# Transformer block on one core: four projections as single f32 products of unsplit operands

## The chip, the cores and the metric

The kernel runs on one core of a Trainium2 chip. The metric is the device time of one execution in microseconds (us). The core has five engines that run side by side and wait for each other through semaphores: TensorE (PE, matrix products; its weight loads are shown as PEld), VectorE (DVE), ScalarE (ACT), GpSimd (POOL) and SyncE (SP, which issues transfers).

## The reference

`x` is 16 x 112 rows of 256 numbers, `ctx` 16 x 375 rows of 192. The block is a cross attention with 16 heads of 16 numbers, followed by a mixture of 8 experts of which each row takes two; both are added to `x` behind a gate.

```python
q = (layernorm(x) @ Wq)            # 16 batches, 112 x 256
k = ctx @ Wk                       # 16 batches, 375 x 256
v = ctx @ Wv
attn = softmax(q @ k.T / 4)        # for each batch and head
x = x + tanh(g_xattn) * ((attn @ v) @ Wo)
# then, for each row of layernorm(x): router, top 2 of 8 experts
y = sum_e probs[e] * ((silu(x @ gate_w[e] + gate_b[e]) * (x @ up_w[e] + up_b[e])) @ down_w[e] + down_b[e])
x = x + tanh(g_ffn) * y
```

The change touches the four products with Wq, Wk, Wv and Wo.

## The kernel before, in words

`build` runs two parts in turn, `attention` and `experts`. Each engine has a program of its own, written out in order; between engines there are only semaphores.

**Two number formats.** TensorE takes 4-byte operands in two ways. As `F32R` (fp32r) a product is one matmul instruction of reduced precision. As `F32` the builder issues two weight loads and two matmul instructions for one `pe.matmul`. The kernel before gets its precision out of fp32r by splitting: an operand is written as a high part (the fp32r copy) and a low part (the operand less its high part), and a product is three: high x high, low x high, high x low. The weights are split once (`w_high` on ACT, `w_low` on DVE, tiles `wk_h`, `wk_l` and so on); the transposed context is split for each batch (`cTH` on ACT, `cTL` on DVE, `transposed`), so are the transposed attention outputs (`oTH`, `oTL`), and the normalised `x` for each group of four batches (`xTH`, `xTL`).

**The start.** SP loads the weights, the first contexts and X. PE projects K and V of batch 0; DVE takes the statistics of X. Then, for four groups of four batches, PE transposes normalised rows into `psO` (`turn`, L687) and multiplies them by Wq (L707: `wq_h` and `wq_l` with `xTH` and `xTL`, 448 columns), ACT copies the results to `qH`, DVE makes `qL`, and SP writes both to `q_scr` in memory. `turn(g + 1)` may write `psO` when `s_xl` says that DVE has read it for `xTL`.

**The steps.** After that come 19 steps, one for each batch and three to drain. Step n projects K and V of batch n (`project_k` L542, `project_v` L552), takes the scores of batch n-1 and their row maxima (`scores` L566 on PE, `maximum` L732 on DVE), takes the transposed scores of batch n-2 again with the maximum subtracted (`scores_T` L581), their exponentials (ACT L468), the low parts of these (`low`: DVE L722 or POOL L346) and their products with V (`sums` L600), multiplies batch n-3 by Wo (`project_o` L637) and routes batch n-4 (L621, L628). A step has 15 slots, and each engine walks through them in this written order: on PE, K stands in slots 1 and 2 (`KP`), V in slots 4 to 6 (`VP`), the transpose of the maxima (`max_T`, L572) in slot 8, the transpose of the next context (`ctx_T` L532) in slot 10, Wo in slot 12.

**The loops between engines.** Scores use two banks in turn, so that `scores` of head h waits for the maximum of head h-2. V shares the tile `misc` with K: `project_v` waits for `v_K`, the end of DVE's `kL` (L786), which follows ACT's `kH` (L481), which follows the second half of K. SP writes `kH` and `kL` to `k_scr` (L271), waits until they have landed and loads them back, arranged by head, as `KS` (L275, 3 transfers of 376 KB). Behind these it issues the row of negative maxima, `nm` (DVE L796 after `max_T`), into `QS` (L304); the first `scores_T` of the next step waits for it:

```python
                    if k == 0:
                        pe.wait_ge(d_m[u], 16 * (h + 1))
```

So one step runs from `max_T` over the slots 9 to 14 (the tail) to the first `scores_T` of the next step, and over its slots 0 to 8 (the head) to the next `max_T`.

## Time and profile before

| | us |
|---|---|
| median of 3 runs | 670.81 |
| lowest and highest of them | 664.48, 671.11 |
| the profiled execution | 665.95 |
| its span, first to last instruction | 664.2 |

The span is one execution as the hardware profiler saw it; 1.75 us of the profiled execution lie outside it. Its stages: the start up to 57 us, the attention steps from 57 to about 366 us, the routing up to 456 us, the tiles of the experts up to the end. The lowest and the highest of the three runs lie 1% apart, and the profiled execution is near the lowest, so a time that is worked out from the profiled execution has to be moved by 4.9 us to stand beside the median.

### The profile page before, as it was taken

The page shows a single profiled execution, that of the slowest core. Times are in us where ns is not written, and L with a number is a line of the kernel's source. Part 1 is how long each engine was busy: PE and PEld are TensorE (multiplying, and loading weights), DVE is VectorE, ACT ScalarE, POOL GpSimd, SP SyncE. Part 2 cuts the span into 40 slices and gives each one's busy share as a digit, 9 for nine tenths or more (in the row PEclk, how much of TensorE's full clock was granted, in tenths as well). Part 3 has the DMA queues.
Part 4 walks back from the last instruction along what each step waited for, and adds up shares of the span by engine and source line. Part 5 has one row for each costly group of instructions (what it writes and reads, how often), then busy time and mean ns, then how long its engine had stood idle before and what let it go on. Part 6 is the DMA issues. An engine that isn't in the chain of part 4 may idle for free. (4 is left out here: it accounts for less than half of the span.)

```text
span 664.2 us, 15005 instructions
## 1 busy us (share of the span) xinstructions
PE 489.1 (74%) x4678; PEld 441.6 (66%) x4679; DVE 428.0 (64%) x896; ACT 329.3 (50%) x600; POOL 290.5 (44%) x238
## 2 busy tenths in 40 slices
PE   3368579898899999899988400004999999999950
PEld 2366478788788888788877300003899999999940
DVE  1755388887789998799888589710555555555520
ACT  1332255666557766657656552501555555555520
POOL 9301255553355555454547037871133333333340
PEclk9998599998899999899989755556999999999995
DMA  8448665688687877767530394934143334333224
GB/s 181 128 101 211 153 146 136 193 236 232 152 228 213 229 175 224 230 175 200 127 84 2 112 349 153 353 100 156 41 65 60 61 62 63 57 58 59 34 33 126
DMA packets 84360, 94.64 MB, mean 143 GB/s; under 512 B 27128, under 2 KB 72912, under 8 KB 84128
## 3 DMA queue, kind: packets, MB, share of 16 engines
q1 hardware_dynamic: 76736, 84.92, 46.5%
q0 software_dynamic: 7584, 9.21, 9.1%
q8 instruction: 23, 0.38, 0.3%
q14 instruction: 17, 0.14, 0.1%
HBM read 60.99 MB, written 34.83 MB: 144 GB/s over the span
## 5 line engine op out<-in xcount | busy, mean ns | idle before, releaser
L346 POOL TENSOR_TENSOR PL<-PT 125x448 f16<-125x448 f32 x96 | 100.3, 1048 | 146.5 <-ACT PT L468 146.4
L732 DVE TENSOR_REDUCE mx<-bank 112x1 f32<-112x375 f32 x256 | 130.6, 542 | 43.5 <-PE bank L566 41.3
L468 ACT ACTIVATE PT<-bank 125x448 f32<-125x448 f32 x192 | 103.8, 544 | 91.3 <-PE bank L581 90.6
L1286 POOL DMA_INDIRECT acc_scr<-ys,where x42 | 65.2, 1552 | 131.9 <-ACT ys L1318 122.9
L566 PE MATMUL bank<-KS,QS 97*112 97x376 f32 x256 | 90.6, 378 | 13.5 <-DVE mx L732 11.0
L581 PE MATMUL bank<-QS,KS 98*125 98x256 f32 x384 | 83.9, 303 | 15.1 <-DMA QS<-nm 14.3
L581 PEld LDWEIGHTS bank<-QS,KS 98*125 98x125 f32 x384 | 66.7, 193 | 17.4 <-DMA QS<-nm 10.2
L1335 PE MATMUL bank<-ident,xt 128*128 128x128 f32 x84 | 13.5, 289 | 71.7 <-PEq L954 71.7
L1349 PE MATMUL bank<-xH,GH 128*128 128x256 f16 x336 | 64.7, 274 | 0.9 <-DVE xL L1381 0.6
L1349 PE MATMUL bank<-xL,GH 128*128 128x256 f16 x336 | 64.6, 274 | 0.0
L1349 PE MATMUL bank<-xH,GL 128*128 128x256 f16 x336 | 64.4, 273 | 0.0
L566 PEld LDWEIGHTS bank<-KS,QS 97*112 97x112 f32 x256 | 46.5, 185 | 25.0 <-DVE mx L732 20.8
L1389 DVE SCALAR_TENSOR_TENSOR hf<-bank,ub,sg 128x256 f32<-128x256 f32 x84 | 38.6, 481 | 38.0 <-ACT sg L1308 38.0
L722 DVE TENSOR_TENSOR PL<-PT 125x448 f16<-125x448 f32 x96 | 57.7, 618 | 3.0 <-ACT PT L468 2.6
L1335 PEld LDWEIGHTS bank<-ident,xt 128*128 128x128 f32 x84 | 10.1, 148 | 72.4 <-DMA xt<-xs_scr 72.0
L1308 ACT ACTIVATE sg<-bank,gb,inv 128x256 f32<-128x256 f32 x84 | 42.7, 559 | 30.2 <-PE bank L1349 30.1
L600 PE MATMUL bank<-VS,PT 125*128 125x49 bf16 x768 | 51.2, 186 | 2.8 <-DVE PL L722 2.1
L600 PE MATMUL bank<-VS,PL 125*128 125x49 bf16 x768 | 49.7, 184 | 0.0
L600 PEld LDWEIGHTS bank<-VS,PT 125*128 125x128 bf16 x768 | 38.7, 99 | 12.7 <-DVE PL L722 2.4
L1037 POOL DMA_INDIRECT xs_scr<-xn,pos x32 | 41.1, 1285 | 10.6 <-issue 7.6
L1393 DVE TENSOR_TENSOR hL<-hf,hH 128x1024 fp32r<-128x1024 f32 x21 | 25.7, 1225 | 23.7 <-ACT hH L1313 23.7
L1318 ACT ACTIVATE ys<-ys,where 128x256 f32<-128x256 f32 x42 | 19.0, 500 | 41.7 <-DVE ys L1401 41.7
(202 smaller groups left out, 1123.7 us busy)
## 6 DMA issues: line engine op xcount, KB each, us to landing
KS<-k_scr SPq DMA_DIRECT2D x48, 376.0 KB
k_scr<-kH SPq DMA_DIRECT2D x16, 376.0 KB, 2.5
k_scr<-kL SPq DMA_DIRECT2D x16, 376.0 KB, 3.7
xs_scr<-empty SPq DMA_DIRECT2D x9, 645.0 KB, 9.0
xt<-xs_scr SPq DMA_DIRECT2D x21, 258.0 KB, 2.8
QS<-q_scr SPq DMA_DIRECT2D x96, 56.0 KB, 5.0
ctx_sb<-in_ctx SPq DMA_DIRECT2D x16, 281.2 KB
wsq<-in_L_ffn_gate_w SPq DMA_DIRECT2D x8, 512.0 KB, 4.6
```

The costliest lines, as they stand in the source:

```text
L346: pool.tensor_tensor(PL[:, 2 * k:2 * k + 2, :, 0:N], PT[:, 2 * k:2 * k + 2, :, 0:N], PH[:, 2 * k:2 * k + 2, :, 0:N], ALU.subtract).then_in ...
L468: act.activation(PT[:, 2 * k:2 * k + 2, :, 0:N].rearrange("p a e i -> p (a e) i"), psST[k % 2][0:JP].rearrange("p (a i) -> p a i", i=NI)[: ...
L566: pe.matmul(psS[hd % 2][0:N, 0:MP], QS[u][0:RM, hd // 2, hd % 2, 0:N], KS[u][0:RM, hd // 2, :], start=True, stop=True).then_inc(p_S, 1)
L581: mm = pe.matmul(psST[k % 2][0:JP, 2 * NI * a:2 * NI * (a + 1)], KS[u][0:RM + 1, p, JP * t:JP * (t + 1)], QS[u][0:RM + 1, p, :, :].rearran ...
L600: mm = pe.matmul(psO[hd // 8][:, VW * (hd % 8):VW * (hd % 8 + 1)], P[:, JT * p + t, e, :], VS[:, u, t, hd, :], start=(part == 0 and t == 0 ...
L722: dve.tensor_tensor(PL[:, 2 * k:2 * k + 2, :, 0:N].rearrange("p a e i -> p (a e) i"), PT[:, 2 * k:2 * k + 2, :, 0:N].rearrange("p a e i -> ...
L732: dve.tensor_reduce(mx[:, hd:hd + 1], psS[hd % 2][0:N, 0:M], AX.X, ALU.max).then_inc(v_max, 1)
L1037: pool.indirect_dma_start(xs_scr, bass.IndirectOffsetOnAxis(ap=pos[k][:, b:b + 1].bitcast(mybir.dt.uint32), axis=0), xn[:, b, :], None).th ...
L1286: pool.indirect_dma_start(acc_scr, bass.IndirectOffsetOnAxis(ap=where[:, t % UN, k, 0:1].bitcast(mybir.dt.uint32), axis=0), ys[:, u, k, :] ...
L1308: act.activation(sg[:, f, :], bG[f // FB][:, TS * (f % FB):TS * (f % FB + 1)], ACT.Silu, bias=gb[:, bass.ds(e * FC + f, 1)], scale=inv[:, ...
L1349: mm = pe.matmul(bank[:, TS * (f % FB):TS * (f % FB + 1)], w.rearrange("p o f -> p (o f)"), x[:, u, k, :], start=(n == 0 and k == 0), stop ...
L1389: dve.scalar_tensor_tensor(out=hf[:, f, :], in0=bU[f // FB][:, TS * (f % FB):TS * (f % FB + 1)], scalar=ub[:, bass.ds(e1 * FC + f, 1)], in ...
```

## The change

The weights stay as loaded, in `Wf`, now kept for the whole of the attention part, and the products take them and the unsplit `cT`, `xT` and `oT` as `F32`. Every product of three pairs of fp32r instructions becomes one of two `pe.matmul` calls (one for each half of the contraction), each of which is issued as two matmul instructions with a weight load each. The splitting steps of ACT and DVE are gone: `w_high`, `w_low`, DVE's `transposed`, `oTL` and `xTL`. PE waits for ACT's copy in their place (`a_T`, `a_O`, `s_xc`), and for the transfers of the weights. The scale 1/4 of the queries moves from the weights to `q_high` and `q_low`, where DVE's subtraction becomes a `scalar_tensor_tensor` of the same size. The split of q and k for the scores stays.

```diff
-        WH = {k: sb(f"w{k}_h", [p, 2, DIM], F32R) for k, (_, p) in shapes.items()}
-        WL = {k: sb(f"w{k}_l", [p, 2, DIM], F32R) for k, (_, p) in shapes.items()}
+        Wf = {k: sb(f"w{k}_f", [p, 2, DIM], F32) for k, (_, p) in shapes.items()}
...
-        cTH = sb("cTH", [CK, 2, MP], F32R)
-        cTL = sb("cTL", [CK, 2, MP], F32R)
+        cT = sb("cT", [CK, 2, MP], F32)
...
-        xTH = first("xTH", [128, 2, 2, GB * N], F32R)
-        xTL = first("xTL", [128, 2, 2, GB * N], F32R)
+        xT = first("xT", [128, 2, 2, GB * N], F32)
...
-        oTH = sb("oTH", [128, 2, N], F32R)
-        oTL = sb("oTL", [128, 2, N], F32R)
+        oT = sb("oT", [128, 2, N], F32)
...
-                def w_high(k):
-                    act.wait_ge(s_w[k], 16)
-                    act.activation(WH[k][:], Wf[k][:], ACT.Copy, scale=SCALE if k == "q" else 1.0).then_inc(s_wh, 1)
...
-                w_high("k")
-                w_high("v")
                 transposed(0, 0)
                 act.wait_ge(s_g, 32)
                 act.activation(tg[:], gates[:], ACT.Tanh).then_inc(s_tg, 1)
-                w_high("q")
-                w_high("o")
...
-                        act.activation(qH[:, g, c, :], (psS, psST)[g % 2][c][:, 0:GB * N], ACT.Copy
-                                       ).then_inc(s_qh, 1)
+                        act.activation(qH[:, g, c, :], (psS, psST)[g % 2][c][:, 0:GB * N], ACT.Copy,
+                                       scale=SCALE).then_inc(s_qh, 1)
...
-                        act.activation(xTH[:, g % 2, c, :], psO[c][:, 0:GB * N], ACT.Copy).then_inc(s_xh, 1)
+                        act.activation(xT[:, g % 2, c, :], psO[c][:, 0:GB * N], ACT.Copy).then_inc(s_xc, 1)
...
-                        pe.wait_ge(v_T, b + 1)
-                    for n, (w, r) in enumerate(((WH, cTH), (WL, cTH), (WH, cTL))):
-                        for k in range(2):
-                            mm = pe.matmul(misc[:, 512 * m:512 * m + MP], w["k"][:, k, m * 128:(m + 1) * 128],
-                                           r[:, k, :], start=(n == 0 and k == 0), stop=(n == 2 and k == 1))
+                        pe.wait_ge(a_T, b + 1)
+                    for k in range(2):
+                        mm = pe.matmul(misc[:, 512 * m:512 * m + MP], Wf["k"][:, k, m * 128:(m + 1) * 128],
+                                       cT[:, k, :], start=(k == 0), stop=(k == 1))
...
-                    for n, (w, r) in enumerate(((WH, cTH), (WL, cTH), (WH, cTL))):
-                        for k in range(2):
-                            mm = pe.matmul(misc[0:JP, DIM * t:DIM * (t + 1)], r[:, k, JP * t:JP * (t + 1)],
-                                           w["v"][:, k, :], start=(n == 0 and k == 0), stop=(n == 2 and k == 1))
+                    for k in range(2):
+                        mm = pe.matmul(misc[0:JP, DIM * t:DIM * (t + 1)], cT[:, k, JP * t:JP * (t + 1)],
+                                       Wf["v"][:, k, :], start=(k == 0), stop=(k == 1))
...
-                    pe.wait_ge(v_O, b + 1)
-                    for n, (w, r) in enumerate(((WH, oTH), (WL, oTH), (WH, oTL))):
-                        for k in range(2):
-                            mm = pe.matmul(psS[0][0:N, 0:DIM], r[:, k, :], w["o"][:, k, :],
-                                           start=(n == 0 and k == 0), stop=(n == 2 and k == 1))
+                    pe.wait_ge(a_O, b + 1)
+                    for k in range(2):
+                        mm = pe.matmul(psS[0][0:N, 0:DIM], oT[:, k, :], Wf["o"][:, k, :], start=(k == 0), stop=(k == 1))
...
-                pe.wait_ge(s_wl, 2)
+                pe.wait_ge(s_w["k"], 16)
+                pe.wait_ge(s_w["v"], 16)
...
-                        pe.wait_ge(s_xl, g)
+                        pe.wait_ge(s_xc, 2 * g)
...
-                pe.wait_ge(s_wl, 3)
+                pe.wait_ge(s_w["q"], 16)
...
-                    pe.wait_ge(s_xl, g + 1)
+                    pe.wait_ge(s_xc, 2 * g + 2)
...
-                        for n, (w, r) in enumerate(((WH, xTH), (WL, xTH), (WH, xTL))):
-                            for c in range(2):
-                                mm = pe.matmul((psS, psST)[g % 2][m][:, 0:GB * N],
-                                               w["q"][:, c, m * 128:(m + 1) * 128], r[:, g % 2, c, :],
-                                               start=(n == 0 and c == 0), stop=(n == 2 and c == 1))
+                        for c in range(2):
+                            mm = pe.matmul((psS, psST)[g % 2][m][:, 0:GB * N], Wf["q"][:, c, m * 128:(m + 1) * 128],
+                                           xT[:, g % 2, c, :], start=(c == 0), stop=(c == 1))
...
-                pe.wait_ge(s_wl, 4)
+                pe.wait_ge(s_w["o"], 16)
...
-                def transposed(i, c):
-                    b, h, u = at(i, c)
-                    dve.wait_ge(a_T, b + 1)
-                    dve.tensor_tensor(cTL[:, :, 0:M], misc[0:CK].rearrange("p (c n) -> p c n", c=2)[:, :, 0:M],
-                                      f32(cTH[:, :, 0:M]), ALU.subtract).then_inc(v_T, 1)
...
-                        if s == OT + 1 and live(i, c, 3):
-                            b, h, u = at(i, c - 3)
-                            dve.wait_ge(a_O, b + 1)
-                            dve.tensor_tensor(oTL[:], psS[0][:, 0:2 * N].rearrange("p (c i) -> p c i", c=2),
-                                              f32(oTH[:]), ALU.subtract).then_inc(v_O, 1)
...
-                        if s == CT + 1 and live(i, c, -1) and not starts(i, c):
-                            transposed(i, c + 1)
...
-                def w_low(k, n):
-                    dve.wait_ge(s_wh, n)
-                    dve.scalar_tensor_tensor(out=WL[k][:], in0=Wf[k][:], scalar=SCALE if k == "q" else 1.0,
-                                             in1=f32(WH[k][:]), op0=ALU.mult, op1=ALU.subtract).then_inc(s_wl, 1)
-
-                w_low("k", 1)
-                w_low("v", 2)
-                transposed(0, 0)
...
-                w_low("q", 3)
-                w_low("o", 4)
...
-                        ins = dve.tensor_tensor(qL[:, g, c, :], (psS, psST)[g % 2][c][:, 0:GB * N],
-                                                f32(qH[:, g, c, :]), ALU.subtract)
+                        ins = dve.scalar_tensor_tensor(out=qL[:, g, c, :], in0=(psS, psST)[g % 2][c][:, 0:GB * N],
+                                                       scalar=SCALE, in1=f32(qH[:, g, c, :]), op0=ALU.mult,
+                                                       op1=ALU.subtract)
...
-                    dve.wait_ge(s_xh, 2 * g + 2)
-                    if g >= 2:
-                        dve.wait_ge(s_qp, g - 1)
-                    for c in range(2):
-                        ins = dve.tensor_tensor(xTL[:, g % 2, c, :], psO[c][:, 0:GB * N], f32(xTH[:, g % 2, c, :]),
-                                                ALU.subtract)
-                    ins.then_inc(s_xl, 1)
...
-                    if g == 1:
-                        transposed(0, 1)
```

On TensorE, in slots 1 and 2 of a step inside the loop: scores and transposed scores between the two halves of K. Before:

```order
L581 MATMUL bank<-QS,KS 125x256 x2
L542 MATMUL misc<-cTH,wk_h 128x376 x2
L542 MATMUL misc<-cTH,wk_l 128x376 x2
L542 MATMUL misc<-cTL,wk_h 128x376 x2
L566 MATMUL bank<-KS,QS 112x376 x2
```

With the change:

```order
L566 MATMUL bank<-QS,KS 125x256 x2
L526 REGISTER_ALU
L528 MATMUL misc<-cT,wk_f 128x376 x2
L232 REGISTER_ALU
L551 MATMUL bank<-KS,QS 112x376
```

Nothing has moved: the three pairs of fp32r products of a half of K are one pair of f32 products at the same place, in front of the same scores.

On VectorE, in the tail of a step inside the loop, from the negative maxima to the update of X. Before:

```order
L796 TENSOR_SCALAR nm<-bank 16x112
...
L746 TENSOR_TENSOR on<-osum,rden 112x128
L776 TENSOR_TENSOR oTL<-bank,oTH 128x224
...
L722 TENSOR_TENSOR PL<-PT 125x4x112
L752 REGISTER_ALU
L753 TENSOR_TENSOR cTL<-misc,cTH 96x2x375
L721 REGISTER_ALU
L722 TENSOR_TENSOR PL<-PT 125x4x112
L801 ISA
```

With the change:

```order
L767 TENSOR_SCALAR nm<-bank 16x112
...
L728 TENSOR_TENSOR on<-osum,rden 112x128
...
L704 TENSOR_TENSOR PL<-PT 125x4x112
L703 REGISTER_ALU
L704 TENSOR_TENSOR PL<-PT 125x4x112
L772 ISA
```

The two subtractions are gone from between the low parts of the exponentials; the rest keeps its order.

## Rows read from the trace of the kernel before

**Rows 1.** The page: busy time of the engines; TensorE's clock in 40 slices.

```profile
PE 489.1 (74%) x4678; PEld 441.6 (66%) x4679; DVE 428.0 (64%) x896; ACT 329.3 (50%) x600; POOL 290.5 (44%) x238
...
PEclk9998599998899999899989755556999999999995
```

**Rows 2.** The instructions of L572, one a step: duration, first and last start.

```profile
L572 PE MATMUL bank<-ident,mx x16: 262/263/354, 70.5 to 353.8; 112*16 112x112 f32 x16
```

**Rows 3.** Busy time by stretches: length, engines, clock, DMA share, GB/s; a tail, a head.

```profile
209.20:214.20 5.00, 4.81 (x75) 4.33 (x75) 4.81 (x12) 3.09 (x8) 1.28 (x1) 1.00 1.08 227
214.20:227.10 12.90, 11.74 (x112) 10.62 (x112) 11.48 (x24) 9.65 (x17) 7.99 (x8) 1.00 0.79 244
```

**Rows 4.** Waits of PE from 137.5 to 299 us: total, times, longest.

```profile
PE bank L566 <- DVE mx L732: 5.0, 15, 0.6
PE bank L581 <- DMA QS<-nm: 4.7, 4, 1.4
```

**Rows 5.** Timeline of PE, half of K and the scores behind it.

```profile
215.14 0.51 PE L542 MATMUL misc<-cTH,wk_h 96*128 96x376 f32 x2
...
215.84 0.50 PE L542 MATMUL misc<-cTL,wk_h 96*128 96x376 f32 x2
216.17 0.50 PE L566 MATMUL bank<-KS,QS 97*112 97x376 f32 x2
```

**Rows 6.** Timeline of PE, third of V and the scores behind it.

```profile
220.06 0.50 PE L552 MATMUL misc<-wv_h,cTH 96*125 96x256 f32 x2
...
220.64 0.40 PE L552 MATMUL misc<-wv_h,cTL 96*125 96x256 f32 x2
220.88 0.34 PE L566 MATMUL bank<-KS,QS 97*112 97x376 f32 x1
```

**Rows 7.** Timeline of DVE, tail and head of one step.

```profile
210.74 0.39 DVE L776 TENSOR_TENSOR oTL<-bank,oTH 128x224 fp32r<-128x224 f32 x1
...
212.17 0.94 DVE L753 TENSOR_TENSOR cTL<-misc,cTH 96x750 fp32r<-96x750 f32 x1
213.02 0.61 DVE L722 TENSOR_TENSOR PL<-PT 125x448 f16<-125x448 f32 x1
...
219.07 0.93 DVE L786 TENSOR_TENSOR kL<-misc,kH 128x752 fp32r<-128x752 f32 x1
...
221.26 1.00 DVE L732 TENSOR_REDUCE mx<-bank 112x1 f32<-112x375 f32 x2 [0.34 <-PE bank L566]
```

**Rows 8.** Timeline: f32 products of the routing; fp32r products at the start.

```profile
13.45 0.83 PE L542 MATMUL misc<-cTH,wk_l 96*128 96x376 f32 x2
...
14.08 0.83 PE L542 MATMUL misc<-cTL,wk_h 96*128 96x376 f32 x2
...
384.29 0.63 PE L1080 MATMUL bank<-r_exp,ones 112*112 112x128 f32 x2
```

**Rows 9.** Groups of PE's instructions by shape: busy time, mean ns of one.

```profile
L1080 PE MATMUL bank<-r_exp,ones 112*112 112x128 f32 x2 | 0.6, 421 | 0.0
```

**Rows 10.** Busy time and clock of the stretch that holds L1080.

```profile
380.00:390.00 10.00, 1.61 (x6) 1.16 (x6) 8.27 (x15) 7.31 (x5) 5.56 (x2) 0.50 1.07 372
```

**Rows 11.** Tile nm: who waited for it (us, times), its transfers from issue to landing.

```profile
  PE bank L581: 14.3, 9
...
DMA to landing us min/median/max: 1.7/4.4/6.6
```

**Rows 12.** Timeline of SP's issues: the loads of KS and nm behind them.

```profile
206.30 1.31 SPq L275 DMA_DIRECT2D KS<-k_scr  x3
209.90 0.56 SPq L304 DMA_DIRECT2D QS<-nm  x1
```

**Rows 13.** Timeline of the start: query products and the wait for xTL.

```profile
40.26 0.56 PE L707 MATMUL bank<-xTH,wq_l 128*128 128x448 f32 x2
...
40.66 0.57 PE L707 MATMUL bank<-xTL,wq_h 128*128 128x448 f32 x2
...
47.39 1.04 PE L687 MATMUL bank<-ident,xn 112*128 112x112 f32 x8 [4.30 <-DVE xTL L864]
```

More of the change, by code:

```diff
@@ L120, in attention @@
         first = lambda name, shape, dt: early.enter_context(nc.sbuf_tensor(name, shape, dt))
-        Wf = {k: first(f"w{k}_f", [p, 2, DIM], F32) for k, (_, p) in shapes.items()}
         mask_sb = first("mask_sb", [B, M], U8)
@@ L148, in attention @@
         s_id0, s_id = sem("ident_zero"), sem("ident_ready")
-        s_clear, s_wh, s_wl, s_bias = sem("cleared"), sem("w_high"), sem("w_low"), sem("bias_ready")
+        s_clear, s_bias = sem("cleared"), sem("bias_ready")
         s_st, s_mv, s_ve, s_sq, s_rs = (sem(n) for n in ("ln_stats", "ln_mv", "ln_veps", "ln_sqrt", "ln_rstd"))
-        s_xn, s_xt, s_xh, s_xl = sem("xn_ready"), sem("xT_ready"), sem("xT_high"), sem("xT_low")
+        s_xn, s_xt, s_xc = sem("xn_ready"), sem("xT_ready"), sem("xT_copied")
         s_qp, s_qh, s_ql = sem("q_psum"), sem("q_high"), sem("q_low")
@@ L176, in attention @@
         a_T, a_K, a_V, a_V1, a_V2, a_E, a_O = (sem(n) for n in ("act_ctxT", "act_k", "act_v", "act_v1", "act_v2", "act_exp", "act_oT"))
-        v_T, v_K, v_L, v_max, v_nm = (sem(n) for n in ("dve_ctxT", "dve_k", "dve_plow", "dve_max", "dve_negmax"))
-        v_os, v_rd, v_on, v_O, v_x1 = (sem(n) for n in ("dve_osum", "dve_rden", "dve_on", "dve_oT", "dve_x1"))
+        v_K, v_L, v_max, v_nm = (sem(n) for n in ("dve_k", "dve_plow", "dve_max", "dve_negmax"))
+        v_os, v_rd, v_on, v_x1 = (sem(n) for n in ("dve_osum", "dve_rden", "dve_on", "dve_x1"))
         g_r, g_V, g_L = (sem(n) for n in ("pool_rest", "pool_v", "pool_plow"))
@@ L237, in wait @@
                 eng.wait_ge(s, value)
-        constants = [(f32(cTH[:, :, M:MP]), 0.0), (f32(cTL[:, :, M:MP]), 0.0), (bias_sb[:, M:MP], 0.0),
+        constants = [(cT[:, :, M:MP], 0.0), (bias_sb[:, M:MP], 0.0),
                      (VS[:, :, :, :, VW - 1:VW].rearrange("p u t h o -> p (u t) h o"), 1.0)]
@@ L405, in transposed @@
                         wait(act, p_V, JT * b)
-                        act.activation(cTH[:, :, 0:M], misc[0:CK].rearrange("p (c n) -> p c n", c=2)[:, :, 0:M],
+                        act.activation(cT[:, :, 0:M], misc[0:CK].rearrange("p (c n) -> p c n", c=2)[:, :, 0:M],
                                        ACT.Copy).then_inc(a_T, 1)
@@ L457, in slots @@
                             wait(act, p_Wo, b)
-                            act.activation(oTH[:], psS[0][:, 0:2 * N].rearrange("p (c i) -> p c i", c=2),
+                            act.activation(oT[:], psS[0][:, 0:2 * N].rearrange("p (c i) -> p c i", c=2),
                                            ACT.Copy).then_inc(a_O, 1)
```

## The prediction

> **What bounds the kernel now.** I read the page first. TensorE is the busiest engine, VectorE stands not far behind, and neither is full [rows 1]. The change touches the start and the attention steps alone; routing and experts run the same code. Then the steps: L572 stands in each once, 16 times from 70.5 to 353.8 us, so a step lasts 283.3 / 15 = 18.9 us [rows 2]. The two stretches of one such step show in its head of 12.9 us 11.74 us of PE and 11.48 us of DVE, in its tail of 5.0 us 4.81 us of each, with the transfer engines full all through the tail (share 1.08) [rows 3]. No single engine bounds it; the question is which hand-over comes last, slot by slot. The waits answer it in part: in 161 us PE waits 15 times for a maximum, 5.0 us in total, and 4 times for the transfer of `nm`, up to 1.4 us [rows 4].
>
> In the tail the transfers decide. The loads of KS are issued at 206.3 us, `nm` behind them at 209.9 us [rows 12]. `nm` is 7 KB and needs a median of 4.4 us to land, up to 6.6; PE waits for it in 9 of 16 steps, 14.3 us in total [rows 11]. In the step of the rows it lands at about 214.1 us, 0.1 us before the first `scores_T`. So in 9 steps the chain kL, k_scr, KS, nm sets when the next head begins, and in the other steps the tail's own work ends at nearly the same time.
>
> In the head PE sets the pace in slots 1, 2 and 4 to 6, where K and V stand in front of the scores. DVE is idle there for 0.34 us until PE has passed a third of V and the score behind it [rows 6, 7].
>
> **The price of an f32 product.** In the routing the second of two f32 products of 128 columns shows 0.63 us for two matmul instructions of 0.421 us each [rows 8, 9], so they follow each other by 0.63 - 0.42 = 0.21 us, at a granted clock of 0.50, 1.2 GHz [rows 10]: 1.64 ns a column. The fp32r products at 13.45 us follow each other by (14.08 - 13.45) / 2 = 0.315 us for 376 columns, 0.84 ns a column [rows 8]; that is 1.8 times what the same product takes at 215 us, so I take PE's clock for halved there too, though the page's row shows no drop. An f32 instruction thus costs two fp32r instructions of the same width, and there are two of it for each `pe.matmul`. Three fp32r products become one that costs four. At full clock:
>
> - K: a pair takes 0.35 us [rows 5], one 0.175. Half of K: 6 x 0.175 = 1.05 us before, 4 x 0.33 to 0.35 = 1.32 to 1.40 with the change. I take +0.30 us for each half, +0.60 for both.
> - V: a pair takes 0.24 us (220.64 to 220.88) [rows 6], one 0.12. A third of V: 0.72 before, 4 x 0.23 = 0.92 with the change: +0.20, three thirds +0.60.
> - Wo: the same width and count as a third of V, +0.20.
> - Wq: a pair takes 0.40 us [rows 13], one 0.20 for 448 columns. A group: 12 x 0.20 = 2.4 before, 8 x 0.39 = 3.1 with the change, +0.7, four groups +2.8.
>
> The Trainium skill says the same by another way, "FP8 and Floating Point Precision", TensorE Precision Notes: a true FP32 product is four passes through the array. By it the four replace three passes, and K's 1.05 us would be an estimated 1.40; the rows above give 1.32 to 1.40.
>
> **What goes.** On DVE, for each step, `oTL` 0.39 us and `cTL` 0.94 us [rows 7], with its successors overlapping by 0.1 each: 1.15 us. At the start, four weight splits, 8 `xTL` and two `cTL`. On ACT four weight copies, which stood beside loads. `oTL` and `cTL` both lie in the tail, not in the head where PE is paced.
>
> **The head of a step.** K's second half ends 0.6 us later, so `kH`, `kL` and V begin 0.6 us later; `kL` starts 219.07 in the step of the rows, behind the maximum of head 5, which itself waits for PE then. V adds 0.2 in each of three slots; DVE, which waited 0.34 us at 221.26 [rows 7], waits longer and has no work to bring forward, since the scores are in PE's order behind V. So the head grows by 1.2 us. Cover for it would be PE's waits for maxima, 5.0 us in 9 steps [rows 4], 0.55 a step; they lie in slots 3, 7 and 8, after the added work, where DVE is the late one. Where DVE was late it now gets its scores 1.2 us later too, so little of this cover counts; I take 0.1 of it: +1.1 us.
>
> **The tail.** DVE's last low part there starts at 213.02, right after `cTL` [rows 7], and the last `sums` wait for it. Without `cTL` they could start 0.4 us earlier. Wo's +0.2 falls before the router, whose input comes from ACT; between 0 and 0.2 of it counts, and I take 0.1. So the tail's own work shrinks by 0.2 to 0.3 us. Where `nm` decides, nothing of this counts, but the chain gives something else: it starts with kL, before V, so V's 0.6 us pass while the transfers run. Such a step grows by K's 0.6 us alone. That gives 9 steps x 0.6 = 5.4 us and 6 steps x (1.1 - 0.25) = 5.1 us: +10.5 us for the 15 steps with K and V.
>
> **The start.** Wq's +2.8 us stands on PE's path to the first scores, V of batch 0 with 18 fp32r instructions at half clock adds 3 x 0.4 = 1.2 us before `turn`. Against it: DVE's splits of wq and wo in front of the first `normal`, by the width of `cTL` (750 columns in 0.94 us [rows 7]) 0.64 us each for 512; `turn(1)` and `turn(3)` wait for ACT's copy and not for `xTL` behind it. PE waits 4.30 us for `xTL` at 47.39 us [rows 13], and that chain (cTL, normal, xTL) loses two of its three DVE steps, some 1 to 2 us. Sum: between -1.5 and +1.5 us, I take 0. In the first steps, up to 93 us, the clock is low (the fifth of the page's 40 slices, 66 to 83 us, stands at 5 tenths, the fourth at 8 [rows 1]), and K and V cost up to double the extra: +1 us, mostly under the first long wait for `nm`.
>
> **Sum.** 665.95 + 10.5 + 0 + 1 = 677.5 us on the profiled execution's own time. That execution lies 4.9 us below the median of the runs shown. Moved by these, the median of the changed kernel should be 682 us, +1.7%.
>
> **The rivals.**
>
> *Hidden in the transfer chain: 674 us (chance 0.24).* All steps are bound by kL, KS and nm, and V is free in all; PE's waits for `nm` are halved in length, so the clock drops after them go as well. Between 83 and 350 us four of the page's slices of 16.6 us stand at 8 tenths where the others have 9 [rows 1]; a tenth of such a slice is 1.7 us. 15 x 0.6 = 9, +1 at the start, less 4 x 1.7 = 6.8: +3 us. For it: transfers are full in the tail, `nm` takes a median of 4.4 us. Against: in 6 of the steps PE had no wait for it.
>
> *DVE's relief decides: 657 us (0.06).* If DVE is the engine that is late in most slots, the 1.15 us that it loses shorten the step: 15 x 1.15 = 17 less, +1 to 4 given back by Wq. For it: 16.3 us of DVE in a step of 17.9 [rows 3]. Against: the 1.15 us lie in the tail, and `nm` would have to land 1 us earlier. It decides if `nm`'s landing after its issue falls under 3.5 us everywhere.
>
> *An f32 instruction is no dearer than an fp32r one: 643 us (0.05).* Then K costs 4 x 0.175 a half and the head loses 2 x 0.35 + 3 x 0.24 = 1.4 us a step, DVE's part comes on top in part: 15 x 1.6 = 24 us, and 4 us of Wq. The rows at half clock speak against it: 0.21 us for 128 columns would have to be 0.11. They are of 112 weights and 128 columns, so a weight load that takes as long could hide a cheaper stream; that is all there is for it. The Trainium skill, "Perfetto Trace Analysis", Engine Utilization, gives FP32_LOW_HIGH half the output rate of the array; read as the rate of the whole product, this is that rival, read as that of each of the two instructions it is my price.
>
> *PE becomes the bound everywhere: 693 us (0.10).* The whole 1.2 us of the head and 0.2 of Wo count in 15 to 18 steps, 22 us, with no relief in the tail, since kL and with it `nm` come later in step: this is the slow side of my own case.
>
> **How the numbers follow.** My case, 682 us, has 0.55: on its own it reaches from 676 to 689. 1% (6.7 us) is about what a measurement of this kernel can tell from no change. Slower by over 1% are my case but for its lowest tenth and the last rival: 0.49 + 0.10, and a fifth of the first rival, 0.05: 0.64. Within 1%: the rest of those two, 0.25. Faster: 0.11. The range 668 to 692 leaves out the two fast rivals and the upper half of the last one.
>
> **What would show it.** Right: K's instructions at L528 follow each other by 0.33 to 0.35 us at full clock, V's by 0.22 to 0.24; DVE's wait for PE in slots 2 and 5 grows by 0.2 to 0.3 each; a step (L572's successor) lasts 0.7 us more on the mean; PE's waits for `nm` shrink. Wrong: a spacing near 0.17 us; steps that grow by more than 1.2 us (then kL has pushed KS into the next step); or a start that ends more than 2 us from 57 us. The clock is the weakest point: PE is busier, so dips may vanish, and each is worth 1 to 2 us.

## The result, and the profile after

| | before | after |
|---|---|---|
| median, us | 668.72 (4 runs, 664.48 to 671.11) | 680.16 (4 runs, 674.51 to 685.33) |
| ratio, 95% interval | | 1.0172 [1.0103, 1.0242] |
| the profiled execution, us | 665.95 | 685.33 |
| its span, us | 664.2 | 683.5 |

The change costs 1.7%, 11.4 us between the medians. A second measurement of the same kernel, beside 17 runs of the kernel before, gave 1.0127 [1.0055, 1.0200], with a median of 677.84 us (6 runs). The profiled execution of the first measurement is the longest of its four and was left out of the ratio, so sums of the whole are made with the profile of the second one, 674.29 us with a span of 672.5.

The page of the kernel after, to be held against [rows 1]:

```profile
PE 517.5 (76%) x4470; PEld 431.7 (63%) x4471; DVE 405.5 (59%) x852; ACT 327.8 (48%) x596; POOL 288.4 (42%) x237
...
PEclk9997599999989999999996855555899999999995
```

PE has 28 us more to do in fewer instructions (21 us in the second measurement), DVE 22.5 us less. The product rows of the attention steps, PE's timeline of after, half of K and a third of V, each with the scores behind it (before: [rows 5, 6]):

```profile
223.04 1.43 PE L528 MATMUL misc<-cT,wk_f 96*128 96x376 f32 x4
224.02 0.79 PE L551 MATMUL bank<-KS,QS 97*112 97x376 f32 x2
...
231.83 1.03 PE L537 MATMUL misc<-wv_f,cT 96*125 96x256 f32 x4
232.51 0.52 PE L551 MATMUL bank<-KS,QS 97*112 97x376 f32 x1
```

A matmul begins before the one ahead of it has ended. One instruction of 376 columns in fp32 lasts 0.48 us by itself, so four of them spaced by s last 0.48 + 3s = 1.43: s = 0.317 us, where an fp32r one took 0.175. For 256 columns (1.03 - 0.38) / 3 = 0.217, where fp32r took 0.12. So half of K costs 1.27 us instead of 1.05 (+0.22), and a third of V 0.87 instead of 0.72 (+0.15).

The same two stretches of a step as in [rows 3], tail and head, with the same columns:

```profile
217.50:222.14 4.64, 4.64 (x74) 4.06 (x74) 3.67 (x10) 3.09 (x8) 1.23 (x1) 1.00 1.01 247
222.14:235.50 13.36, 12.62 (x108) 10.06 (x104) 11.12 (x24) 9.65 (x17) 8.00 (x8) 1.00 0.73 208
```

The tail has lost 0.36 us and DVE's work in it 1.14; the head is 0.46 us longer and PE's work in it 0.88. This step takes 18.00 us where the one of before took 17.90. DVE's timeline shows what stands where the relief was (before: [rows 7]):

```profile
218.96 1.15 DVE L704 TENSOR_TENSOR PL<-PT 125x448 f16<-125x448 f32 x2
220.85 0.62 DVE L704 TENSOR_TENSOR PL<-PT 125x448 f16<-125x448 f32 x1 [0.73 <-ACT PT L463]
...
229.78 1.00 DVE L714 TENSOR_REDUCE mx<-bank 112x1 f32<-112x375 f32 x2 [0.49 <-PE bank L551]
```

Where `cTL` stood DVE now waits 0.73 us for ACT's exponentials. In the head its wait for a third of V has grown from 0.34 to 0.49 us, by what that third costs.

That the head grew by 0.46 us and not by 0.88 has another reason, on DVE in slot 7: `xc`, the centring of a routed batch, beside POOL's low part, before and then after.

```profile
224.47 0.94 POOL L346 TENSOR_TENSOR PL<-PT 125x448 f16<-125x448 f32 x1 [0.26 <-ACT PT L468]
...
224.71 0.84 DVE L765 TENSOR_SCALAR xc<-X,mv 112x256 f32 x1
```

```profile
232.85 0.93 POOL L341 TENSOR_TENSOR PL<-PT 125x448 f16<-125x448 f32 x1 [0.25 <-ACT PT L463]
...
233.54 0.39 DVE L741 TENSOR_SCALAR xc<-X,mv 112x256 f32 x1
```

From the start of the head to `xc` it was 10.51 us and is 11.40: PE's added work counts in full. Then `xc`, which began 0.24 us behind POOL's instruction and took 0.84 us, begins 0.69 behind it and takes 0.39, and gives 0.45 us back. (The 0.34 us that `xc` takes in some other steps is its shortest.)

But the steps together grew by more than this one. The maxima's transposes, one a step, of after and then of its second measurement (before: [rows 2]):

```profile
L557 PE MATMUL bank<-ident,mx x16: 263/264/356, 71.9 to 370.8; 112*16 112x112 f32 x16
```

```profile
L557 PE MATMUL bank<-ident,mx x16: 263/263/356, 70.4 to 364.7; 112*16 112x112 f32 x16
```

15 steps take 298.9 and 294.3 us where they took 283.3: +1.0 and +0.7 a step. The tile `nm` of after (before: [rows 11]) shows PE's waits for it as they were:

```profile
  PE bank L566: 15.7, 9
...
DMA to landing us min/median/max: 1.8/4.2/7.0
```

And the start, from PE's timeline of after (before: [rows 13]): the wait for `xTL`, 4.30 us, has become one of 1.84 for ACT's copy, and the steps' first scores stand at 55.51 us, 1.6 before those of the kernel before (57.07).

```profile
46.26 0.96 PE L671 MATMUL bank<-ident,xn 112*128 112x112 f32 x8 [1.84 <-ACT xT L503]
...
55.51 0.96 PE L551 MATMUL bank<-KS,QS 97*112 97x376 f32 x2 [2.26 <-DVE qL L809]
```

### The profile page after: what moved, and what is told of

It is laid out like the page before. It is cut to its first block and busy times, and to the rows that moved or that the text cites. A ratio compares the mean times of both kernels' runs of the same rounds, so it can differ in the third digit from the quotient of the medians.

```text
span 683.5 us, 14536 instructions
## 1 busy us (share of the span) xinstructions
PE 517.5 (76%) x4470; PEld 431.7 (63%) x4471; DVE 405.5 (59%) x852; ACT 327.8 (48%) x596; POOL 288.4 (42%) x237
## 5 line engine op out<-in xcount | busy, mean ns | idle before, releaser
L551 PE MATMUL bank<-KS,QS 97*112 97x376 f32 x256 | 109.5, 451 | 13.7 <-DVE mx L714 10.5
L566 PE MATMUL bank<-QS,KS 98*125 98x256 f32 x384 | 86.9, 312 | 16.3 <-DMA QS<-nm 15.7
L566 PEld LDWEIGHTS bank<-QS,KS 98*125 98x125 f32 x384 | 69.1, 201 | 22.0 <-DMA QS<-nm 11.7
L537 PE MATMUL misc<-wv_f,cT 96*125 96x256 f32 x192 | 55.8, 418 | 10.4 <-DVE kL L757 9.1
L528 PE MATMUL misc<-cT,wk_f 96*128 96x376 f32 x128 | 55.0, 561 | 1.0 <-ACT cT L401 1.0
L585 PEld LDWEIGHTS bank<-VS,PT 125*128 125x128 bf16 x768 | 40.2, 102 | 11.8 <-issue 2.1
L537 PEld LDWEIGHTS misc<-wv_f,cT 96*125 96x125 f32 x192 | 35.8, 200 | 17.1 <-DVE kL L757 13.3
```

Of the source, the lines that this page charges most:

```text
L528: mm = pe.matmul(misc[:, 512 * m:512 * m + MP], Wf["k"][:, k, m * 128:(m + 1) * 128], cT[:, k, :], start=(k == 0), stop=(k == 1))
L537: mm = pe.matmul(misc[0:JP, DIM * t:DIM * (t + 1)], cT[:, k, JP * t:JP * (t + 1)], Wf["v"][:, k, :], start=(k == 0), stop=(k == 1))
L551: pe.matmul(psS[hd % 2][0:N, 0:MP], QS[u][0:RM, hd // 2, hd % 2, 0:N], KS[u][0:RM, hd // 2, :], start=True, stop=True).then_inc(p_S, 1)
L566: mm = pe.matmul(psST[k % 2][0:JP, 2 * NI * a:2 * NI * (a + 1)], KS[u][0:RM + 1, p, JP * t:JP * (t + 1)], QS[u][0:RM + 1, p, :, :].rearran ...
L585: mm = pe.matmul(psO[hd // 8][:, VW * (hd % 8):VW * (hd % 8 + 1)], P[:, JT * p + t, e, :], VS[:, u, t, hd, :], start=(part == 0 and t == 0 ...
```

## The experiments

For each profiled run the table has the start up to the first transpose of the maxima, the 15 steps up to the last one, the rest of the span, and the ratio of the timed runs to the kernel before. "Before" and "after" stand for the kernel that was edited. A single profile stands behind each row: where nothing differs, the rest still lies between 307.8 and 313.6, and the 15 steps of after and after_again, the same kernel, differ by 4.6 us. A difference of a few us between two rows of steps shows nothing by itself.

| run | start | 15 steps | rest | ratio, 95% interval |
|---|---|---|---|---|
| before | 70.5 | 283.3 | 310.4 | |
| after | 71.9 | 298.9 | 312.7 | 1.0172 [1.0103, 1.0242] |
| after_again | 70.4 | 294.3 | 307.8 | 1.0127 [1.0055, 1.0200] |
| dve_relief (before) | 66.9 | 280.8 | 311.6 | 0.9906 [0.9862, 0.9950] |
| pe_price (after) | 69.2 | 292.1 | 310.8 | 1.0121 [1.0049, 1.0192] |
| one_product (before) | 56.4 | 289.6 | 311.6 | 0.9892 [0.9822, 0.9962] |
| ks_cut_before | 71.1 | 266.9 | 310.9 | 0.9756 [0.9692, 0.9819] |
| ks_cut_after | 71.9 | 276.9 | 308.6 | 0.9803 [0.9725, 0.9881] |
| f32_k (before) | 69.1 | 284.5 | 310.6 | 1.0060 [1.0018, 1.0103] |
| kv_split (before) | 71.1 | 284.4 | 312.1 | 0.9967 [0.9928, 1.0006] |
| f32_v (before) | 73.0 | 291.3 | 310.2 | 1.0209 [1.0107, 1.0312] |
| nm_act_before | 70.1 | 330.2 | 313.6 | 1.0698 [1.0587, 1.0810] |
| nm_act_after | 71.3 | 329.4 | 310.6 | 1.0548 [1.0381, 1.0715] |
| after_xc9 | 70.8 | 288.0 | 311.3 | 1.0046 [1.0004, 1.0089] |

**after_again**: the changed kernel, measured a second time beside the next three.

> The changed kernel once more, for a ratio with a narrower interval and a second trace of it. Theory (K and V pace the heads, the transfer of nm ends the tails): 1.012 to 1.022 times the kernel before, steps 0.7 us longer on the mean, and the steps without a wait for nm longer by less than 0.7 us, since in the first trace one of them grew by 0.1 us only. Rival (the change is worth nothing, the 1.7% were scatter): under 1.007.

**dve_relief**: the change's relief of DVE without its cost on PE. `cTL`, `oTL` and `xTL` are not made, PE waits for ACT's copies (`v_O` and `s_xl` are replaced in the same way), and the weights' low parts stay.

```diff
-                    pe.wait_ge(v_T, b + 1)
-                    for n, (w, r) in enumerate(((WH, cTH), (WL, cTH), (WH, cTL))):
+                    pe.wait_ge(a_T, b + 1)
+                    for n, (w, r) in enumerate(((WH, cTH), (WL, cTH), (WH, cTH))):
```

> The kernel before, with VectorE's subtractions cTL, oTL and xTL left out; the third product of each projection takes the high part in place of the low one, so TensorE's work is that of before (the low parts are missing from the result). This is the relief of VectorE alone. Theory: nothing in the tails where nm ends them, 0.25 us in the others, and 2 to 3 us at the start, where turn waits for xTL: 3 to 5 us less than before, ratio 0.993 to 0.996. Rival (VectorE decides the steps): 15 x 1.15 = 17 us less, ratio 0.975.

**pe_price**: the change's cost on PE, with two of DVE's subtractions kept and PE waiting for them as before (`oTL` with `v_O` in the same way as `cTL`).

```diff
-                        pe.wait_ge(a_T, b + 1)
+                        pe.wait_ge(v_T, b + 1)
...
+                    dve.tensor_tensor(cTL[:, :, 0:M], misc[0:CK].rearrange("p (c n) -> p c n", c=2)[:, :, 0:M],
+                                      cT[:, :, 0:M], ALU.subtract).then_inc(v_T, 1)
```

> The changed kernel with VectorE's subtractions of the context and of the attention outputs put back (into tiles that nobody multiplies), and TensorE waiting for them as before; the f32 products stay. This is TensorE's price with the steps' relief of VectorE taken away. Theory: the relief in the steps was worth 1 to 3 us, so it is 1.018 to 1.025 times the kernel before. Rival (VectorE decides the steps): 17 us on top of the changed kernel, 1.042.

The transposes of the maxima, of dve_relief and of pe_price:

```profile
L572 PE MATMUL bank<-ident,mx x16: 263/264/354, 66.9 to 347.7; 112*16 112x112 f32 x16
```

```profile
L560 PE MATMUL bank<-ident,mx x16: 263/264/356, 69.2 to 361.3; 112*16 112x112 f32 x16
```

By the timed runs dve_relief is 0.9% faster, 6.3 us (3.4 to 9.3), somewhat more than the 3 to 5 us expected. In its profile 3.6 us of it lie in the start; the steps are shorter by 0.17 us each (280.8 against 283.3), which is within what two profiles of one kernel differ by. Giving 1.3 us of work in each step back to DVE in the changed kernel costs nothing: pe_price is 1.012 where the changed kernel beside it is 1.013, and the 1 to 3 us that I had expected the relief of the steps to be worth did not show. What the change costs in the steps comes from PE's side.

**one_product**: PE's products of all four projections cut to a third; no low parts are made for them.

```diff
-                    for n, (w, r) in enumerate(((WH, cTH), (WL, cTH), (WH, cTL))):
+                    for n, (w, r) in enumerate(((WH, cTH),)):
```

> The kernel before with one fp32r product of the high parts in place of three (the low parts are left out of the result), and no low parts made. TensorE loses 2.7 us of K and V in each head and 0.5 us of Wo in the tail, VectorE 1.15 us. Theory: the heads fall to what VectorE's 11.5 us allow, 1.0 to 1.4 us less a step, the tails stay with the transfer of nm, and the start loses 4 us: 19 to 25 us less than before, ratio 0.963 to 0.972. Rival (TensorE alone is the bound): 15 x 3.3 = 50 us less, 0.925. Rival (the transfers are the bound of every step, from kL to nm): K alone counts, 15 x 1.37 = 20 us, which does not tell from the theory by the time; the trace tells, by the waits for nm.

The page's clock of one_product, and its busy time in the first step and in the 14 behind it (columns as in [rows 3]):

```profile
PEclk9985577858959777969966655556999999999985
```

```profile
56.40:84.90 28.50, 15.92 (x99) 13.84 (x99) 10.54 (x21) 11.39 (x17) 15.20 (x14) 0.52 0.63 157
84.90:346.00 261.10, 234.13 (x2250) 198.83 (x2250) 212.05 (x458) 165.76 (x326) 136.24 (x113) 0.79 0.69 184
```

and the same 14 steps of the kernel before:

```profile
92.40:353.80 261.40, 233.75 (x2564) 209.62 (x2564) 224.41 (x484) 164.81 (x326) 132.62 (x113) 0.97 0.70 185
```

The start gains 14.1 us, of which the first step gives 6.6 back in a wait of PE for ACT's copy of V. The other 14 steps take 261.1 us instead of 261.4, with 314 matmul instructions less: PE is busy just as long, since its granted clock has fallen from 0.97 to 0.79. So PE's work is no simple price either: with a part of it taken out, the clock was lower. I had expected 19 to 25 us less than before, and it was 7 (0.9892).

**ks_cut_before, ks_cut_after**: two of the three transfers that load KS are left out in both kernels.

```diff
-                    for s, part in enumerate((0, 0, 1)):
+                    for s, part in enumerate((0,)):
...
-                        pe.wait_ge(d_ks[u], 64 * (h + 1))
+                        pe.wait_ge(d_ks[u], 32 * (h + 1))
```

> The kernel before with two of the three loads of KS from k_scr left out in each step (752 of 1128 KB; their rows keep the ones of the start, so the scores are others). The transfers between kL and nm get shorter. Theory (the loads of KS hold nm back, and nm ends the tail in half of the steps): no waits for nm after the first, steps of 17.5 to 18 us throughout, 12 to 18 us less than before, ratio 0.973 to 0.982. Rival (the transfers are beside the point, the long steps come from TensorE's clock): the long steps stay, within 4 us of before.

> The changed kernel with the same two loads of KS left out. With the transfers out of the way only what the engines do can differ between the kernels. Theory: the steps differ by what the undisturbed steps of the traces show, 0.1 to 0.7 us each, and the start by 1.5 us less, so the time is 0 to 9 us over that of ks_cut_before. Rival (TensorE's 1.1 us counts in full in every head): 15 us over it.

The tile `nm` of ks_cut_before, and then its transposes of the maxima and those of ks_cut_after:

```profile
  PE bank L581: 2.4, 1
...
DMA to landing us min/median/max: 1.7/1.8/3.1
```

```profile
L572 PE MATMUL bank<-ident,mx x16: 262/263/264, 71.1 to 338.0; 112*16 112x112 f32 x16
```

```profile
L557 PE MATMUL bank<-ident,mx x16: 262/263/280, 71.9 to 348.8; 112*16 112x112 f32 x16
```

Two things follow. The chain behind KS is real: without two thirds of it `nm` lands in 1.8 us instead of 4.4, PE waits for it once, and the kernel before gains 2.4%. And the change does not hide behind it: with the chain out of the way the 15 steps of the profiles still grow by 10.0 us, as they do with it (11.0 in after_again). The timed runs, four of each, agree in the sign only: 657.51 against 652.11 us, with ratios whose intervals meet. The cause had to be elsewhere, and these two profiles, where almost no wait for `nm` blurs the steps, show where. Three of the 15 steps, each third one inside the loop, grow from 17.38 to 19.35 us, together 5.9 of the 10.0. Of the other twelve ten change by -0.95 to +0.5, and two grow by 1.6 and 1.5. One of the three, busy time by stretches, in ks_cut_before and then in ks_cut_after:

```profile
158.80:176.20 17.40, 16.54 (x188) 14.84 (x188) 15.82 (x36) 11.09 (x23) 9.90 (x9) 1.00 0.54 158
```

```profile
160.80:180.10 19.30, 17.26 (x175) 14.12 (x175) 15.99 (x34) 11.07 (x23) 10.57 (x9) 1.00 0.49 134
```

DVE has two instructions less, yet it is busy for 0.17 us longer. One of its instructions has grown.

**f32_k, f32_v**: the kernel before with K alone, or V alone, as one f32 product of the high parts; every splitting step stays.

```diff
-                    for n, (w, r) in enumerate(((WH, cTH), (WL, cTH), (WH, cTL))):
-                        for k in range(2):
...
+                    for k in range(2):
+                        mm = pe.matmul(misc[:, 512 * m:512 * m + MP], f32(WH["k"][:, k, m * 128:(m + 1) * 128]),
+                                       f32(cTH[:, k, :]), start=(k == 0), stop=(k == 1))
```

> The kernel before with K alone as one f32 product, of the high parts (the low parts of K are left out of the result); all of VectorE's work stays, V, Wo and Wq stay split. TensorE spends 2 x 0.23 us more in each head, before kL. Theory: K stands in front of the chain kL, KS, nm and so counts in every step: 15 x 0.46 = 7 us, ratio 1.007 to 1.012, that is the larger half of the change. Rival (any work of TensorE counts alike, K as V): 5 us or less, with V the same.

> The kernel before with V alone as one f32 product, of the high parts (the low parts of V are left out of the result); all else as before. TensorE spends 3 x 0.15 us more in each head, behind kL. Theory: V passes while the loads of KS run, so it counts only in the steps that do not wait for nm: 2 to 4 us, ratio 1.001 to 1.006, less than K's 1.006. Rival (work of TensorE counts alike wherever it stands): as much as K, 1.006 or more.

This refuted my theory that V hides behind the transfers. V alone costs 2.1% (1.1 to 3.1) by the timed runs, and 8.0 us in the 15 steps of its profile, though it adds only 3 x 0.15 us of work to a step. That K counts is not refuted: its profile has 1.2 us more in the steps, but its timed runs 0.6% (0.2 to 1.0), 4 us. The instruction that has grown is `xc`, in slot 7, just behind the last third of V. Its instructions in f32_k and then in f32_v (shortest, median and longest in ns):

```profile
L764 DVE TENSOR_SCALAR xc<-X,mv x16: 344/808/1765, 126.5 to 373.0; 112x256 f32 x9, 112x256 f32<-112x256 f32 x7
```

```profile
L764 DVE TENSOR_SCALAR xc<-X,mv x16: 343/396/1712, 132.0 to 383.7; 112x256 f32 x9, 112x256 f32<-112x256 f32 x7
```

The median falls, and that is a gain in the steps it stands for, but it hides the few long ones: in the three steps `xc` takes 0.34 us in f32_k and 1.70 in f32_v. The kernels before and after show the same. One of these steps on DVE and POOL, of before:

```profile
187.36 0.94 POOL L346 TENSOR_TENSOR PL<-PT 125x448 f16<-125x448 f32 x1 [0.32 <-ACT PT L468]
187.72 0.55 DVE L732 TENSOR_REDUCE mx<-bank 112x1 f32<-112x375 f32 x1 [0.30 <-PE bank L566]
...
188.19 0.34 DVE L765 TENSOR_SCALAR xc<-X,mv 112x256 f32 x1
...
188.25 1.77 POOL L363 TENSOR_TENSOR VS<-vr,VS 125x768 bf16<-125x768 f32 x1
```

and of after:

```profile
192.70 0.55 DVE L714 TENSOR_REDUCE mx<-bank 112x1 f32<-112x375 f32 x1 [0.44 <-PE bank L551]
...
193.08 1.64 POOL L358 TENSOR_TENSOR VS<-vr,VS 125x768 bf16<-125x768 f32 x1
...
193.16 1.70 DVE L741 TENSOR_SCALAR xc<-X,mv 112x256 f32 x1
...
194.79 0.54 DVE L714 TENSOR_REDUCE mx<-bank 112x1 f32<-112x375 f32 x1
```

POOL starts the last of V's casts (`VS`) as soon as its low part is through; DVE starts `xc` as soon as the maximum is, which waits for PE. Before, DVE is 0.06 us ahead and `xc` takes 0.34 us. After, its wait for PE has grown from 0.30 to 0.44 us, by the 0.15 us of a third of V, DVE is 0.08 us behind, and `xc` ends 0.14 us after POOL's instruction. The next maximum, and PE's scores behind it, come 1.4 us later for it. The Trainium skill, "SBUF — State Buffer", Who interferes with whom, has the rule: VectorE and GpSimd share a pair of ports, a `tensor_scalar` that runs in a two-port mode takes it for its whole length, and the one that comes second is blocked until the first is through. The rows agree in the times, both ways round (POOL's 1.77 us behind `xc`, 1.64 ahead of it); that `xc` runs in such a mode no row shows.

So V's delay moves `xc` against POOL's instructions both ways, and the sum has to be taken over all 15 steps. In the ks_cut pair, `xc` and what stands behind it up to the next transpose of the maxima lose 0.41 to 0.47 us in eight steps and gain 1.36 in the three: +0.4 us in all, with -0.1 in the last two. The stretch from the transpose of the maxima to `xc`, with the tail and with K and V, is longer by 0.56 to 0.64 us in eight of the steps, and by 9.6 us over the 15 (the first two, which have no `xc`, counted whole). In the kernels with their transfers the same split is 14.4 + 1.2 us for after and 10.3 + 0.7 for after_again, waits for `nm` included. The larger part of the cost is PE's work in front of the scores, in every step; `xc` costs little on balance.

In two steps of the pair the stretch before `xc` grew by 2.0 and 1.9 us and not by 0.6. They are the two that grew by 1.6 and 1.5 in all, and each stands directly behind a long `xc`. One of them, its busy time in ks_cut_before and ks_cut_after; then, in ks_cut_after, the end of PE's wait ahead of it and two microseconds in it:

```profile
229.85:248.13 18.28, 16.82 (x187) 14.91 (x187) 16.38 (x36) 12.73 (x25) 9.26 (x9) 1.00 0.58 174
```

```profile
236.05:255.94 19.89, 19.16 (x176) 15.64 (x176) 15.03 (x34) 12.84 (x25) 8.01 (x8) 0.91 0.62 176
```

```profile
234.99 0.43 PE L551 MATMUL bank<-KS,QS 97*112 97x376 f32 x1 [1.42 <-DVE mx L714]
```

```profile
237.00:239.00 2.00, 2.00 (x20) 1.88 (x20) 1.69 (x4) 1.25 (x3) 0.00 (x0) 0.50 0.02 4
```

PE had waited 1.42 us for the maximum behind `xc`, and in the tail that followed its granted clock stood at 0.50, 1.2 GHz, for a while. In after, after_again and ks_cut_after eight of the nine steps directly behind one of the three have a mean clock of 0.84 to 0.94, where the same steps of before and ks_cut_before have 1.00; in pe_price and f32_v it is one of three each. The two in the pair cost 1.3 to 1.4 us each beyond the usual 0.6. That the long `xc` brings the lower clock about is argued from this.

**kv_split**: Wq and Wo as in the changed kernel, K and V split as before.

```diff
+        Wf = {k: sb(f"w{k}_f", [shapes[k][1], 2, DIM], F32) for k in "qo"}
...
+                    for k in range(2):
+                        mm = pe.matmul(psS[0][0:N, 0:DIM], oT[:, k, :], Wf["o"][:, k, :], start=(k == 0), stop=(k == 1))
```

> K and V split as before, Wq and Wo as single f32 products as in the changed kernel, xTL, oTL and the splits of wq and wo gone. Theory: the start loses 1.5 us (turn waits for one copy in place of a copy and a subtraction), the steps nothing, since Wo lies in the tail: 0 to 3 us less than before, ratio 0.995 to 1.0. Rival (Wo's 0.15 us and Wq's 2.8 us count): 1.005.

Of the kernels that keep the projections' precision it is the fastest, but 0.9967 [0.9928, 1.0006], within what I had expected, does not show it faster than before. Wo's 0.15 us in slot 12 costs nothing that shows: the steps take 284.4 us.

**nm_act_before, nm_act_after**: `nm` is issued from ACT's queue, in slot 9, and not from SP's behind KS.

```diff
-                        sp.wait_ge(v_nm, b + 1)
-                        sp.dma_start(f32(QS[u][RM:RM + 1, :, :, 0:N]).rearrange("o q e i -> o (q e) i"),
...
+                        if k == MT + 1 and live(i, c, 1):
+                            act.wait_ge(v_nm, b + 1)
+                            act.dma_start(f32(QS[u][RM:RM + 1, :, :, 0:N]).rearrange("o q e i -> o (q e) i"),
...
```

> The kernel before with the transfer of nm issued from ScalarE's queue in place of SyncE's, so that it need not stand behind the loads of KS in the same queue. Theory (what ends the long tails is the loads of KS; the first scores of the next step need KS too): nm lands 1 to 2 us sooner, the waits go over from nm to KS, and the time stays within 3 us. Rival (nm itself is what is late): its waits, 14 us with the first, 8 us without, go: 0.98 to 0.988.

> The changed kernel with nm issued from ScalarE's queue. Theory: as with the kernel before, within 3 us of the changed kernel (1.010 to 1.017 times the kernel before). Rival (nm itself is late): 0.995 to 1.003.

Both became 5 to 7% slower where I had expected a change within 3 us. The tile `nm` of nm_act_before, and then the issues of its SP and its ACT around one `nm`:

```profile
  PE bank L581: 27.7, 13
...
DMA to landing us min/median/max: 1.7/6.2/8.0
```

```profile
248.94 1.31 SPq L275 DMA_DIRECT2D KS<-k_scr  x3
250.46 0.29 SPq L251 DMA_DIRECT2D ctx_sb<-in_ctx  x1
250.96 0.42 SPq L295 DMA_DIRECT2D xs_scr<-empty  x1
```

```profile
253.13 0.52 ACTq L431 DMA_DIRECT2D QS<-nm  x1
```

SP's wait for `nm` had held its later transfers back. Without it the next context and a block of `xs_scr` go out right behind KS and ahead of `nm`, which then lands after 6.2 us instead of 4.4, and PE waits 27.7 us for it, in 13 steps, instead of 14.3 in 9 [rows 11]. The order of issue is what the rows show; that this traffic is what delays `nm` is argued from it. That the two ratios differ by 1.5% doesn't tell the kernels apart, since their intervals meet and their steps take the same time.

**after_xc9**: the changed kernel, with `xc` moved from slot 7 to slot 9 and nothing else. This takes away what the theory names, the long `xc` in three heads. It also takes the short one out of the other heads.

```diff
-        ST, AG, XC, XT, LG, RT = 5, 14, 7, 11, 12, 13
+        ST, AG, XC, XT, LG, RT = 5, 14, 9, 11, 12, 13
```

> The changed kernel with VectorE's center (xc, a subtraction from SBUF to SBUF) moved from slot 7 of the head to slot 9, in the tail, where GpSimd has no work; nothing else. In the traces of every kernel with V as f32 this instruction takes 1.70 us in each third step and 0.39 in the others; where V is split it takes 0.35 in each third step and 0.84 in the others; those third steps are the ones that grew by 1.4 to 2 us. Theory (V's delay makes xc start just behind a GpSimd instruction, and DVE waits for that instruction's end): xc takes 0.35 us in all steps of the loop, the third steps fall by 1.4 us or more and the others by some 0.3, 6 to 12 us less than the changed kernel, 0.997 to 1.005 times the kernel before. Rival (TensorE's f32 time in the heads costs this, xc only fills a wait for it): within 3 us of the changed kernel, 1.011 to 1.018.

Its `xc`, its transposes of the maxima, and `xc` in one step on POOL and DVE:

```profile
L741 DVE TENSOR_SCALAR xc<-X,mv x16: 347/834/1019, 130.6 to 380.1; 112x256 f32 x9, 112x256 f32<-112x256 f32 x7
```

```profile
L557 PE MATMUL bank<-ident,mx x16: 263/264/353, 70.8 to 358.8; 112*16 112x112 f32 x16
```

```profile
248.70 1.32 POOL L341 TENSOR_TENSOR PL<-PT 125x448 f16<-125x448 f32 x1
...
249.32 0.84 DVE L741 TENSOR_SCALAR xc<-X,mv 112x256 f32 x1
```

The long ones are gone, and the ratio falls to 1.0046 [1.0004, 1.0089], below the whole interval of the change's first measurement and below the value of the second, 1.0127, whose interval it meets. The steps take 288.0 us: 6.3 less than in after_again, 10.9 less than in after, and 4.7 more than before. Two of the three steps that stood behind a long `xc` have their clock of 1.00 again. So moving `xc` is worth some 6 us to the changed kernel. It doesn't say how much of the change's cost is `xc`'s, since the kernel before, which has an `xc` of some 0.8 us in most of its heads, was not run with it moved. `xc` did not become short, as I had expected: in slot 9 it meets POOL's low part and takes 0.84 us nearly everywhere.

## Why the prediction was right, and where it was not

The time was predicted at 682 us and measured at 680.16, with a ratio of 1.017 where 1.017 was forecast. The cause that it named, PE's f32 products in front of the scores of each head, carries most of the cost. That the number came out to 0.3% was luck: the terms were too large, others were missing, and the second measurement gave 1.0127.

- **The price of an f32 instruction**: right. It is twice that of an fp32r one (0.317 against 0.175 us, 0.217 against 0.12). The terms were somewhat large: +0.22 for half of K where I took +0.30, and +0.15 for a third of V where I took +0.20, since I had rounded the spacing up. The rival of 643 us is refuted. The Trainium skill's halved rate ("Perfetto Trace Analysis", Engine Utilization) is by these rows that of each instruction, so that a whole product costs four.
- **The head, +1.1 us**: the mechanism held, its size did not. I had PE's added work at 1.2 us, and it measured 0.88. That PE's waits for DVE cover next to none of it was right up to `xc`: that stretch of the head grew by 0.89 us in the step of the rows. Behind it the shorter `xc` gave 0.45 back, so that the head grew by 0.46. With the shorter tail, eight steps of the ks_cut pair grow by 0.56 to 0.64 up to `xc`, where my mean for a step was 0.7; 15 times 0.6 would be 9 us, an estimate, where my sum had 10.5.
- **What was missing**: `xc` beside POOL, with +1.36 us in three steps and -0.45 in eight, together 0.4 to 1.2 us in the pairs of profiles; and the lower clock in the steps behind the long ones, 2.7 us in the ks_cut pair. Nothing in my working looked at DVE's SBUF instructions beside POOL's. The row was there to be found: before, the same instruction takes 0.34 us in some steps, 0.84 in most and 1.76 once.
- **In the steps that `nm` decides only K's 0.6 us counts, V is hidden**: wrong. V alone costs 2.1%, clearly more than K alone with its 0.6%, and as much as the whole change within the noise.
- **The tail**: -0.36 us, a little more than the 0.2 to 0.3 I gave it. DVE's 1.3 us bought no time that shows in the steps, about as predicted (pe_price, the steps of dve_relief); its rival of 657 us is refuted.
- **The start, 0 within -1.5 and +1.5**: a miss to the fast side, -1.6 us in after and -3.0 in after_again up to the first scores (54.03 us there). By my own list a start more than 2 us from 57 was a sign of being wrong, and one of the two is. The first head, at a mean clock of 0.69, gave it back: 13.4 us before, 16.4 in both profiles after, +3.0, where I had +1 for all the steps at the low clock. f32_v, which keeps the splits and pays for V at the start, is 2.5 us later than before at the first maxima, which may be one reason why V alone is no cheaper than the whole change (their intervals meet).
- **PE's waits for `nm` shrink**: not so in after (15.7 us, 9 times), somewhat in after_again (10.8 us, 8 times). "Hidden in the transfer chain" fell with the profiles of the ks_cut pair: the chain is there, but the steps grow as much without it.

Open: why V alone costs as much as the whole change; where the 15 steps of two profiles of one kernel get their 4.6 us of scatter (waits for `nm`, the clock); the scatter of the span behind the steps, up to 5.8 us between kernels that run nearly the same code there; and whether the kernel before, or kv_split, gains as well by `xc` moved, which was not run. No complete version was shown to beat it.

## What to carry to other kernels

An added 0.15 us turned 0.34 us into 1.70 in three steps here, and 0.84 into 0.39 in eight: in a written-out schedule look, for each DVE instruction that reads and writes SBUF beside GpSimd, at who starts first and by how little, and look at its duration step by step. Take the sum over all steps before you call such a thing the cause: the long ones stand out, and the short ones paid for most of them. Test a theory about which part of a change costs with each part alone; here the total was forecast well and V's share in it wrongly. And before a wait is taken out of a queue, list what it has been holding back.

## What the hardware did that I had not expected

- Two instructions of 0.34 and 1.64 us, 0.08 us apart in the wrong order, took 1.70 us on DVE; in the right order, 0.06 us apart, 0.34.
- PE waited 1.42 us behind such an instruction, and in the next tail its granted clock stood at 0.50; the step took 19.89 us instead of 18.28. Eight of nine such waits in the changed kernel (with and without the cut of KS) had a step with a lower clock behind them.
- With two thirds of the projections' products gone, 14 attention steps took 261.1 us instead of 261.4, at a granted clock of 0.79 instead of 0.97.
- A transfer of 7 KB from another engine's queue did not get past the traffic of SP's: median 6.2 us from issue to landing, against 4.4 behind it and 1.8 where two thirds of the KS loads are left out.
